# A selective scan whose step sizes return from DRAM already spread, in place of a spreading matmul

## The chip, the cores and the metric

One core of a Trainium2 chip. The metric is the device time of one execution in microseconds (us); lower is better.

## The reference

Eight images of 32x32 tokens with 192 channels pass through four residual blocks: attention with rotary positions (A), a selective scan (B), attention with relative positions (C) and 7x7 neighbourhood attention (D). The change is in B. What B computes, cut to the part that matters:

```python
x_dbl = jnp.einsum('bkdl,kcd->bkcl', xs, x_proj_w)        # xs: 4 directions over the 1024 tokens, 96 channels
dts, Bs, Cs = jnp.split(x_dbl, [R, R + N], axis=2)        # N = 16 states
dts = jax.nn.softplus(jnp.einsum('bkrl,kdr->bkdl', dts, dt_projs_w) + dt_projs_b[None, :, :, None])
def step(h, inp):                                          # over the 1024 tokens
    u_t, d_t, B_t, C_t = inp
    dA = jnp.exp(d_t[..., None] * As)
    h = h * dA + (d_t * u_t)[..., None] * B_t[:, :, None, :]
    y = jnp.einsum('bkcn,bkn->bkc', h, C_t)
```

## The kernel before

The four blocks run one after the other. In B the images also run one after the other. An image has a head (normalization, input projection, a 3x3 convolution, gates, then dt, B and C of the first direction), 48 tiles, and a tail (the sum over directions, a layer norm, a gate, the output projection).

A tile is 8 channels by 16 states on the 128 partitions, and all 1024 steps of the scan along the free axis. The 96 channels make 12 tiles for each direction k = 0 to 3; tile i has k, j = divmod(i, 12). For each tile:

- TensorE copies each of 8 rows of dt to 16 partitions (`spread_dt`, L1206 to L1219) into one of two slots of PSUM (`m.s2`), and the same for dt*u (`spread_du`, L1221 to L1230) into the single slot `m.s1`. A row is first split into a rounded part and a rest (`dth`, `duh`), so a spread has two parts and two halves: four matmuls.
- ScalarE takes the exponential of the spread dt in place in PSUM (L1376).
- VectorE multiplies the spread dt*u by B into `m.hs` in SBUF (`input_term`, L1478), then runs the scan (L1489): `h = h * dA + input`, with dA read from PSUM and the input from `hs`, written over `hs`.
- GpSimd multiplies the states by C (L1533) from SBUF into `m.hc`; every three tiles TensorE sums the 16 states back to channels in `m.px` (`fold`, L1232 to L1245).

The order on each engine is the program's order. VectorE runs `input_term(i + 1)` ahead of the scan of tile i. TensorE runs `spread_dt(i)`, waits until `input_term(i)` has emptied `m.s1`, and then runs `spread_du(i + 1)`; a slot of `m.s2` comes free when the scan that read it has ended. Between the tiles of direction k the work for direction k + 1 is threaded in: three projections on TensorE (tiles 0 to 5, also through `m.s1`), softplus on ScalarE (tiles 0 to 4) and on VectorE: `correct` (L1433) behind the scan of tile 5, `tail` (L1438) behind tile 6, `floor` (L1443) behind tile 7, `softplus` (L1448) and `scaled` (L1456, dt*u) behind tile 8, `low_dt` (L1461) behind tile 9, `low_du` (L1467) behind tile 10. All of these read two tensors from SBUF. ScalarE's `high_dt` and `high_du` (L1354, L1359) make the rounded parts. `m.dt` and `m.du` are the two halves of `m.xn`. SyncE's queue holds in B only the loads and stores of whole images.

Of the kernel before, what the change touches and what calls it, by code (L numbers as in the profile page):

```python
# [172 lines left out]
class ScanSignals:  # L173
    def __init__(self, sem, L):
# [23 lines left out]
        self.dt_ps = sem(f"{L}_dt_ps")  # L198
# [15 lines left out]
def allocate(nc, ctx):  # L214
# [106 lines left out]
    with ExitStack() as scan:  # L321
        m.dth = [sb(scan, f"dth{i}", [CP, 2, N], F32R) for i in range(2)]
# [862 lines left out]
def scan_image_tensor(nc, pe, m, b):  # L1185
# [20 lines left out]
    def spread_dt(i):  # L1206

        k, j = divmod(i, NG)
        if j == 0:
            pe.wait_ge(s.dt_lo, KD * b + k + 1)  # L1210
        if i == 1:
            pe.wait_ge(s.z_used, b + 1)
        if i >= 2:
            pe.wait_ge(s.h, TILES * b + i - 1)
        for f in range(NHF):
            for part in range(2):
                last = nc.tensor.matmul(m.s2[:, i % 2, f * HF:(f + 1) * HF], m.spread[:, ORDER[j], :],  # L1217
                                        m.dth[k % 2][:, part, f * HF:(f + 1) * HF], start=part == 0, stop=part == 1)
        last.then_inc(s.dt_ps, 1)  # L1219

    def spread_du(i, halves):  # L1221

        k, j = divmod(i, NG)
        if j == 0:
            pe.wait_ge(s.du_lo, KD * b + k + 1)
        for f in halves:
            for part in range(2):
                last = nc.tensor.matmul(m.s1[:, f, :], m.spread[:, ORDER[j], :],  # L1228
                                        m.duh[k % 2][:, part, f * HF:(f + 1) * HF], start=part == 0, stop=part == 1)
            last.then_inc(s.du_ps, 1)  # L1230
# [25 lines left out]
    spread_du(0, (0, 1))  # L1256
    for i in range(TILES):
        k, j = divmod(i, NG)
        spread_dt(i)
        pe.wait_ge(s.bt, TILES * b + i + 1)  # L1260
        f, ahead = j % 2, NHF * (KD * b + k + 1) + j % 2 + 1
        if k + 1 < KD and j < 2:
            project(k + 1, m.wdt, CP, f, s.dtp_ps)
            spread_du(i + 1, (1 - f,))
            pe.wait_ge(s.dtp_used, ahead)
            spread_du(i + 1, (f,))
        elif k + 1 < KD and j < 4:
            project(k + 1, m.xbw, P, f, s.brep_ps)
            spread_du(i + 1, (1 - f,))
            pe.wait_ge(s.brep, ahead)  # L1270
            spread_du(i + 1, (f,))
        elif k + 1 < KD and j < 6:
            project(k + 1, m.xcw, P, f, s.crep_ps)
            spread_du(i + 1, (1 - f,))
            pe.wait_ge(s.crep, ahead)
            spread_du(i + 1, (f,))
        elif i + 1 < TILES:
            spread_du(i + 1, (0, 1))
# [24 lines left out]
def scan_image_scalar(nc, act, m, b):  # L1303
# [64 lines left out]
    high_dt(0)  # L1368
# [3 lines left out]
    for i in range(TILES):  # L1372
        k, j = divmod(i, NG)
        act.wait_ge(s.dt_ps, TILES * b + i + 1)
        g = NG * k + ORDER[j]
        nc.scalar.activation(m.s2[:, i % 2, :], m.s2[:, i % 2, :], ACT.Exp,  # L1376
# [13 lines left out]
        if k + 1 < KD and j == 8:  # L1390
            high_dt(k + 1)
# [349 lines left out]
```

## Time and profile before

| | |
|---|---|
| median of 3 runs | 8861.15 us (8851.8 to 8868.71) |
| the profiled execution | 8870.59 us, span 8868.8 us, mean granted TensorE clock 0.864 |
| block B in it | the first scan at 1946.5, the last at 4528.6 us |
| one image of B | 334 us, of which 244.3 us from its first scan's start to its last scan's start |
| the scan instruction, L1489 | 384 times, 2277 ns each |
| GpSimd's multiply, L1533 | 384 times, 2551 ns each |

The span runs from the first to the last instruction. A row of the timeline has the start in us from the span's start, the duration in us, engine, line, operation and tiles; in brackets the idle time of the engine before it and who ended it. When an instruction had to wait for something that the profile doesn't record as a wait, its duration grows.

### The profile page before, as it was taken

How to read it: one execution, taken by the hardware profiler on the slowest of the kernel's cores; microseconds unless marked ns; L12 is line 12 of the kernel's file. 1: busy time of each engine (PE TensorE's matmuls, PEld its weight loads, DVE VectorE, ACT ScalarE, POOL GpSimd, SP SyncE). 2: the span in 40 equal slices, each digit the busy share in tenths (PEclk: the TensorE clock that was granted, in tenths of full speed). 3: DMA queues.
4: the chain of work that ended last, by engine and by line, in shares of the span. 5: the costliest groups of instructions: out<-in, count | busy, mean ns of one | idle time of the engine just before them, and what ended most of it. 6: DMA issues, size and time to landing. Idle time of an engine off the chain costs nothing. (4 is left out here: it accounts for less than half of the span.)

```text
span 8868.8 us, 86314 instructions
## 1 busy us (share of the span) xinstructions
PE 7117.3 (80%) x32664; PEld 2841.9 (32%) x32664; DVE 5281.6 (60%) x5310; ACT 3280.4 (37%) x3610; POOL 1168.2 (13%) x468
## 2 busy tenths in 40 slices
PE   6888888867777777777779999999989996777776
PEld 2222222223223223233234343344333432333332
DVE  5777777757777767777765555555555553333333
ACT  2555555532323322322323343333433432222222
POOL 0000000014334334334320000000000000000000
PEclk9999999988878778778778999999989997888787
DMA  2111111100000000000001001111010101222221
GB/s 65 47 46 48 48 48 48 46 23 0 7 7 0 7 7 0 7 7 0 4 29 29 27 29 35 29 30 30 27 35 27 30 25 54 65 66 62 64 68 46
DMA packets 152812, 282.83 MB, mean 32 GB/s; under 512 B 46858, under 2 KB 53762, under 8 KB 152398
## 3 DMA queue, kind: packets, MB, share of 16 engines
q1 hardware_dynamic: 152398, 277.31, 10.8%
q8 instruction: 260, 4.26, 0.2%
q14 instruction: 154, 1.26, 0.0%
HBM read 165.34 MB, written 89.79 MB: 29 GB/s over the span
## 5 line engine op out<-in xcount | busy, mean ns | idle before, releaser
L927 DVE TENSOR_REDUCE mx<-ring 128x1 f32<-128x1024 f32 (+1 forms) x1920 | 2187.8, 1141 | 2536.0 <-PE ring L674 1255.0
L825 ACT ACTIVATE pt<-ring 128x1024 f32<-128x1024 f32 (+1 forms) x1920 | 1868.4, 981 | 2836.0 <-PE ring L700 1329.5
L724 PE MATMUL px<-pt,vo 128*32 128x512 f32 (+3 forms) x8064 | 1277.2, 616 | 9.5 <-ACT pt L825 9.3
L671 PE MATMUL ring<-kb,qb 96*128 96x512 bf16 x3072 | 1121.2, 407 | 203.0 <-DVE rq L912 96.2
L698 PE MATMUL ring<-qb,kb 99*128 99x512 bf16 x3072 | 1124.0, 408 | 161.7 <-DVE nb L947 67.9
L1533 POOL TENSOR_TENSOR hc<-hs,crep 128x1024 f32<-128x1024 f32 x384 | 979.7, 2551 | 1684.0 <-DVE hs L1489 1593.7
L1228 PE MATMUL ring<-duh,spread 96*128 96x512 f32 x1536 | 650.7, 537 | 362.0 <-DVE hs L1478 230.5
L1489 DVE TENSOR_TENSOR_SCAN hs<-ring,hs 128x1024 f32<-128x1024 f32 x384 | 874.5, 2277 | 2.1 <-ACT ring L1376 2.1
L700 PE MATMUL ring<-rq,hot 128*128 128x512 f32 x1536 | 865.5, 622 | 0.0
L674 PE MATMUL ring<-hot,rq 128*128 128x512 f32 x1536 | 856.6, 616 | 0.0
L1376 ACT ACTIVATE ring<-ring,arow 128x1024 f32<-128x1024 f32 x384 | 415.9, 1083 | 947.8 <-PE ring L1217 947.8
L698 PEld LDWEIGHTS ring<-qb,kb 99*128 99x128 bf16 x3072 | 266.7, 100 | 1319.9 <-issue 684.5
L1478 DVE TENSOR_TENSOR hs<-ring,brep 128x1024 f32<-128x1024 f32 x384 | 467.3, 1217 | 358.8 <-PE ring L1228 312.6
L671 PEld LDWEIGHTS ring<-kb,qb 96*128 96x128 bf16 x3072 | 280.7, 100 | 907.0 <-issue 396.5
L1217 PE MATMUL ring<-dth,spread 96*128 96x512 f32 x1536 | 521.1, 467 | 30.4 <-DVE hs L1489 29.6
L667 PE MATMUL ring<-ks,qs 112*128 112x320 f32 x768 | 270.4, 441 | 330.5 <-DMA ks<-qk_split 295.2
L1228 PEld LDWEIGHTS ring<-duh,spread 96*128 96x128 f32 x1536 | 307.3, 218 | 699.8 <-DVE hs L1478 298.8
L1243 PE MATMUL px<-hc,fold 128*32 128x512 f32 x1536 | 476.0, 1018 | 31.8 <-POOL hc L1533 30.9
L1217 PEld LDWEIGHTS ring<-dth,spread 96*128 96x128 f32 x1536 | 313.4, 221 | 480.6 <-issue 346.4
L1030 POOL TENSOR_TENSOR ocn<-ocm,rb 96x1024 f32<-96x1024 f32 x24 | 56.7, 2362 | 2717.1 <-DMA rb<-reciprocals 2388.0
L1030 POOL TENSOR_TENSOR ocm<-ocm,rb 96x1024 f32<-96x1024 f32 x24 | 56.4, 2351 | 2428.2 <-DMA rb<-reciprocals 2428.2
L667 PEld LDWEIGHTS ring<-ks,qs 112*128 112x128 f32 x768 | 147.2, 234 | 609.5 <-issue 505.4
(169 smaller groups left out, 6792.5 us busy)
## 6 DMA issues: line engine op xcount, KB each, us to landing
qk_parts<-part SPq DMA_DIRECT2D x192, 192.0 KB, 2.4
qb<-qk_parts SPq DMA_DIRECT2D x192, 96.0 KB
kb<-qk_parts SPq DMA_DIRECT2D x192, 96.0 KB
ocm<-os SPq DMA_DIRECT2D x576, 32.0 KB
rb<-reciprocals SPq DMA_DIRECT2D x288, 64.0 KB, 2.5
qb<-qk_parts SPq DMA_DIRECT2D x192, 64.0 KB
kb<-qk_parts SPq DMA_DIRECT2D x192, 64.0 KB
qk_split<-hi SPq DMA_DIRECT2D x32, 384.0 KB, 3.5
```

What stands on the lines that cost most here:

```text
L671: last = nc.tensor.matmul(out[:, half], m.qb[u][0:BR, q], m.kb[u][0:BR, half], start=True, stop=L == "A")
L674: last = nc.tensor.matmul(out[:, half], m.rq[u][:, q], m.hot[:, half], start=False, stop=True)
L698: last = nc.tensor.matmul(out[:, half], m.kb[u][:, k], m.qb[u][:, half], start=True, stop=L == "A")
L700: last = nc.tensor.matmul(out[:, half], m.hot[:, k], m.rq[u][:, half], start=False, stop=True)
L724: last = nc.tensor.matmul(m.px[32 * g:32 * g + 32, h % 2, lo - f * HF:hi - f * HF], m.vo[img % 2][:, t, VW * head:VW * head + VC], pt[:, l ...
L825: nc.scalar.activation(pt, ps, ACT.Exp, scale=1.0 if L == "C" else HD ** -0.5).then_inc(s.pt, 1)
L927: nc.vector.tensor_reduce(out, ps, AX.X, ALU.max).then_inc(s.mx_used, 1)
L1217: last = nc.tensor.matmul(m.s2[:, i % 2, f * HF:(f + 1) * HF], m.spread[:, ORDER[j], :], m.dth[k % 2][:, part, f * HF:(f + 1) * HF], start ...
L1228: last = nc.tensor.matmul(m.s1[:, f, :], m.spread[:, ORDER[j], :], m.duh[k % 2][:, part, f * HF:(f + 1) * HF], start=part == 0, stop=part ...
L1243: last = nc.tensor.matmul(m.px[32 * band:32 * (band + 1), f, :], m.fold[:, v, :], rhs, start=False, stop=t >= TILES - BANDS, skip_group_ch ...
L1489: nc.vector.tensor_tensor_scan(m.hs[i % HSS][:], m.s2[:, i % 2, :], m.hs[i % HSS][:], 0.0, ALU.mult, ALU.add).then_inc(s.h, 1)
L1533: nc.gpsimd.tensor_tensor(m.hc[i % HCS][:], m.hs[i % HSS][:], m.crep[k % 2][:], ALU.mult).then_inc(s.hc, 1)
```

## The change

The spread of dt leaves TensorE. When softplus of a direction is done, SyncE writes dt (96 rows of 1024, 384 KB) to an internal DRAM tensor, waits until it has landed, and then issues one load for each tile: 8 rows, each read 16 times, 512 KB to 128 partitions of one of four new SBUF buffers `dts`. The load of tile i waits for the scan of tile i - 4. ScalarE's exponential works in place on `dts` in SBUF, and the scan reads dA from there. `high_dt`, `low_dt` and the buffers `dth` are gone; `low_du` moves from behind tile 10 to behind tile 9. The spread of dt*u takes over the two slots of `m.s2` and runs two tiles ahead; `m.s1` is left to the projections, which now wait only for the copy two projections back.

```diff
+DTS = 4
-        m.dth = [sb(scan, f"dth{i}", [CP, 2, N], F32R) for i in range(2)]
+        m.dts = [sb(scan, f"dts{i}", [P, N]) for i in range(DTS)]
+    m.dtd = nc.dram_tensor("dt_rows", (2, CP, N), F32, kind="Internal").ap()
...
-    def spread_dt(i):
+    def spread_du(i):
         k, j = divmod(i, NG)
         if j == 0:
-            pe.wait_ge(s.dt_lo, KD * b + k + 1)
+            pe.wait_ge(s.du_lo, KD * b + k + 1)
         if i == 1:
             pe.wait_ge(s.z_used, b + 1)
         if i >= 2:
-            pe.wait_ge(s.h, TILES * b + i - 1)
+            pe.wait_ge(s.bt, TILES * b + i - 1)
         for f in range(NHF):
             for part in range(2):
                 last = nc.tensor.matmul(m.s2[:, i % 2, f * HF:(f + 1) * HF], m.spread[:, ORDER[j], :],
-                                        m.dth[k % 2][:, part, f * HF:(f + 1) * HF], start=part == 0, stop=part == 1)
-        last.then_inc(s.dt_ps, 1)
-    def spread_du(i, halves):
...
                                         m.duh[k % 2][:, part, f * HF:(f + 1) * HF], start=part == 0, stop=part == 1)
-            last.then_inc(s.du_ps, 1)
+        last.then_inc(s.du_ps, 1)
...
-    spread_du(0, (0, 1))
+    for i in range(2):
+        spread_du(i)
     for i in range(TILES):
         k, j = divmod(i, NG)
-        spread_dt(i)
-        pe.wait_ge(s.bt, TILES * b + i + 1)
-        f, ahead = j % 2, NHF * (KD * b + k + 1) + j % 2 + 1
+        f, back = j % 2, NHF * (KD * b + k) + j % 2 + 1
         if k + 1 < KD and j < 2:
+            pe.wait_ge(s.crep, back)
             project(k + 1, m.wdt, CP, f, s.dtp_ps)
-            spread_du(i + 1, (1 - f,))
-            pe.wait_ge(s.dtp_used, ahead)
-            spread_du(i + 1, (f,))
         elif k + 1 < KD and j < 4:
+            pe.wait_ge(s.dtp_used, back + NHF)
             project(k + 1, m.xbw, P, f, s.brep_ps)
...
+        if i + 2 < TILES:
+            spread_du(i + 2)
...
-        act.wait_ge(s.dt_ps, TILES * b + i + 1)
+        act.wait_ge(s.dt_in[i % DTS], 16 * ((TILES * b + i) // DTS + 1))
         g = NG * k + ORDER[j]
-        nc.scalar.activation(m.s2[:, i % 2, :], m.s2[:, i % 2, :], ACT.Exp,
+        nc.scalar.activation(m.dts[i % DTS][:], m.dts[i % DTS][:], ACT.Exp,
                              scale=m.arow[:, g:g + 1]).then_inc(s.da, 1)
...
-        nc.vector.tensor_tensor(m.hs[i % HSS][:], flat(m.s1[:]), m.brep[k % 2][:], ALU.mult).then_inc(s.bt, 1)
+        nc.vector.tensor_tensor(m.hs[i % HSS][:], m.s2[:, i % 2, :], m.brep[k % 2][:], ALU.mult).then_inc(s.bt, 1)
...
-        nc.vector.tensor_tensor_scan(m.hs[i % HSS][:], m.s2[:, i % 2, :], m.hs[i % HSS][:], 0.0,
+        nc.vector.tensor_tensor_scan(m.hs[i % HSS][:], m.dts[i % DTS][:], m.hs[i % HSS][:], 0.0,
                                      ALU.mult, ALU.add).then_inc(s.h, 1)
...
         if k + 1 < KD and j == 9:
-            low_dt(k + 1)
-        if k + 1 < KD and j == 10:
             low_du(k + 1)
...
+        for i in range(TILES):
+            k, j = divmod(i, NG)
+            if j == 0:
+                sp.wait_ge(s.soft, 2 * (KD * b + k) + 1)
+                sp.dma_start(m.dtd[k % 2], m.dt[:]).then_inc(s.dt_out, 16)
+                sp.wait_ge(s.dt_out, 16 * (KD * b + k + 1))
+            if TILES * b + i >= DTS:
+                sp.wait_ge(s.h, TILES * b + i - DTS + 1)
+            rows = m.dtd[k % 2, DB * ORDER[j]:DB * (ORDER[j] + 1), :].rearrange("(d o) n -> d o n", o=1)
+            sp.dma_start(m.dts[i % DTS][:], rows.broadcast_to([DB, NS, N])).then_inc(s.dt_in[i % DTS], 16)
```

## Rows read from the trace of the kernel before

**Rows 1.** Windows, first image's tiles: us, busy of each engine, clock, DMA share, GB/s
```profile
1946.40:2190.70 244.30, 198.42 (x582) 85.84 (x582) 203.41 (x116) 80.91 (x85) 117.96 (x47) 0.83 0.00 0
```

**Rows 2.** Waits in the stretch 1940 to 2200: us in total, times, longest
```profile
DVE hs L1478 <- PE ring L1228: 38.9, 23, 3.6
```

**Rows 3.** Groups by line and shape, 1890 to 4250, the removed spread of dt
```profile
L1217 PE MATMUL ring<-dth,spread 96*128 96x512 f32 x1344 | 455.5, 467 | 26.8 <-DVE hs L1489 26.1
```

**Rows 4.** Timeline of the fourth direction, two scans beside a GpSimd multiply
```profile
2158.38 2.40 POOL L1533 TENSOR_TENSOR hc<-hs,crep 128x1024 f32<-128x1024 f32 x1 [0.85 <-DVE hs L1489]
...
2159.34 2.28 DVE L1489 TENSOR_TENSOR_SCAN hs<-ring,hs 128x1024 f32<-128x1024 f32 x1
...
2162.65 2.28 DVE L1489 TENSOR_TENSOR_SCAN hs<-ring,hs 128x1024 f32<-128x1024 f32 x1
```

**Rows 5.** Timeline of the first direction, tiles 5 to 9 and VectorE's work between them
```profile
1971.19 2.28 DVE L1489 TENSOR_TENSOR_SCAN hs<-ring,hs 128x1024 f32<-128x1024 f32 x1
...
1973.38 1.20 DVE L1433 SCALAR_TENSOR_TENSOR t<-t 96x1024 f32<-96x1024 f32 x1
...
1973.55 3.25 POOL L1533 TENSOR_TENSOR hc<-hs,crep 128x1024 f32<-128x1024 f32 x1 [2.88 <-DVE hs L1489]
...
1975.64 2.27 DVE L1489 TENSOR_TENSOR_SCAN hs<-ring,hs 128x1024 f32<-128x1024 f32 x1
...
1977.99 2.37 POOL L1533 TENSOR_TENSOR hc<-hs,crep 128x1024 f32<-128x1024 f32 x1 [1.19 <-DVE hs L1489]
1978.00 3.43 DVE L1438 TENSOR_TENSOR xn<-xn,t 96x1024 f32<-96x1024 f32 x1
...
1982.50 2.27 DVE L1489 TENSOR_TENSOR_SCAN hs<-ring,hs 128x1024 f32<-128x1024 f32 x1
...
1989.34 2.27 DVE L1489 TENSOR_TENSOR_SCAN hs<-ring,hs 128x1024 f32<-128x1024 f32 x1
...
1998.21 2.27 DVE L1489 TENSOR_TENSOR_SCAN hs<-ring,hs 128x1024 f32<-128x1024 f32 x1
```

**Rows 6.** Timeline of the second direction, the scans of its tiles 8 and 9
```profile
2055.57 2.27 DVE L1489 TENSOR_TENSOR_SCAN hs<-ring,hs 128x1024 f32<-128x1024 f32 x1
...
2063.73 2.27 DVE L1489 TENSOR_TENSOR_SCAN hs<-ring,hs 128x1024 f32<-128x1024 f32 x1
```

**Rows 7.** Timeline: scan of tiles 12, 36 and 47, and the copy that opens the tail
```profile
2014.71 2.28 DVE L1489 TENSOR_TENSOR_SCAN hs<-ring,hs 128x1024 f32<-128x1024 f32 x1
...
2152.71 2.28 DVE L1489 TENSOR_TENSOR_SCAN hs<-ring,hs 128x1024 f32<-128x1024 f32 x1
...
2190.68 2.29 DVE L1489 TENSOR_TENSOR_SCAN hs<-ring,hs 128x1024 f32<-128x1024 f32 x1 [0.27 <-ACT ring L1376]
...
2199.80 1.22 DVE L1506 COPY t<-px 96x1024 f32<-96x1024 f32 x1 [6.82 <-PE px L1243]
```

**Rows 8.** Timeline of the first image's head: softplus, a spread, a projection, the first scan
```profile
1932.69 1.22 DVE L1448 TENSOR_TENSOR xn<-xn 96x1024 f32<-96x1024 f32 x1
...
1938.31 2.05 PE L1228 MATMUL ring<-duh,spread 96*128 96x512 f32 x4 [4.75 <-DVE duh L1467]
...
1941.86 1.90 PE L1203 MATMUL ring<-u,wdt 96*96 96x512 f32 x2
...
1946.45 2.28 DVE L1489 TENSOR_TENSOR_SCAN hs<-ring,hs 128x1024 f32<-128x1024 f32 x1
```

**Rows 9.** DMA issues: KB each, median us from issue to landing
```profile
rb<-reciprocals SPq DMA_DIRECT2D x288, 64.0 KB, 2.5
...
qk_split<-hi SPq DMA_DIRECT2D x32, 384.0 KB, 3.5
...
x<-x_A SPq DMA_DIRECT2D x8, 768.0 KB, 5.4
```

**Rows 10.** Timeline of the first image's tail: two matmul groups of equal size
```profile
2201.07 1.96 PE L1287 MATMUL ring<-t,mean 96*96 96x512 f32 x4 [1.32 <-DVE t L1506]
...
2205.63 3.73 PE L1291 MATMUL ring<-xn,mean 96*96 96x512 f32 x4 [2.60 <-DVE xn L1511]
```

More of the change, by code:

```diff
@@ L189, in __init__ @@
         self.soft = sem(f"{L}_soft")
-        self.dt_hi = sem(f"{L}_dt_hi")
+        self.dt_out = sem(f"{L}_dt_out")
+        self.dt_in = [sem(f"{L}_dt_in{i}") for i in range(DTS)]
         self.du_hi = sem(f"{L}_du_hi")
-        self.dt_lo = sem(f"{L}_dt_lo")
         self.du_lo = sem(f"{L}_du_lo")
@@ L1217, in spread_dt @@
                 last = nc.tensor.matmul(m.s2[:, i % 2, f * HF:(f + 1) * HF], m.spread[:, ORDER[j], :],
-                                        m.dth[k % 2][:, part, f * HF:(f + 1) * HF], start=part == 0, stop=part == 1)
-        last.then_inc(s.dt_ps, 1)
-    def spread_du(i, halves):
[L1223 to L1228, printed above, removed]
                                         m.duh[k % 2][:, part, f * HF:(f + 1) * HF], start=part == 0, stop=part == 1)
-            last.then_inc(s.du_ps, 1)
+        last.then_inc(s.du_ps, 1)
     def fold(i, f):
@@ L1255, in scan_image_tensor @@
     pe.wait_ge(s.crep, NHF * KD * b + NHF)
-    spread_du(0, (0, 1))
+    for i in range(2):
+        spread_du(i)
     for i in range(TILES):
         k, j = divmod(i, NG)
-        spread_dt(i)
-        pe.wait_ge(s.bt, TILES * b + i + 1)
-        f, ahead = j % 2, NHF * (KD * b + k + 1) + j % 2 + 1
+        f, back = j % 2, NHF * (KD * b + k) + j % 2 + 1
         if k + 1 < KD and j < 2:
+            pe.wait_ge(s.crep, back)
             project(k + 1, m.wdt, CP, f, s.dtp_ps)
-            spread_du(i + 1, (1 - f,))
-            pe.wait_ge(s.dtp_used, ahead)
-            spread_du(i + 1, (f,))
         elif k + 1 < KD and j < 4:
+            pe.wait_ge(s.dtp_used, back + NHF)
             project(k + 1, m.xbw, P, f, s.brep_ps)
-            spread_du(i + 1, (1 - f,))
-            pe.wait_ge(s.brep, ahead)
-            spread_du(i + 1, (f,))
         elif k + 1 < KD and j < 6:
+            pe.wait_ge(s.brep, back + NHF)
             project(k + 1, m.xcw, P, f, s.crep_ps)
[L1274 to L1278, printed above, removed]
+        if i + 2 < TILES:
+            spread_du(i + 2)
         if i > BANDS and i % BANDS == 1:
@@ L1367, in scan_image_scalar @@
         copy_b(0, f)
-    high_dt(0)
     for f in range(NHF):
@@ L1389, in scan_image_scalar @@
             logarithm(k + 1)
-        if k + 1 < KD and j == 8:
-            high_dt(k + 1)
         if k + 1 < KD and j == 9:
@@ L1474, in input_term @@
             dve.wait_ge(s.brep, NHF * (KD * b + k + 1))
-        dve.wait_ge(s.du_ps, NHF * (TILES * b + i + 1))
+        dve.wait_ge(s.du_ps, TILES * b + i + 1)
         if i >= HSS:
             dve.wait_ge(s.hc, TILES * b + i - HSS + 1)
-        nc.vector.tensor_tensor(m.hs[i % HSS][:], flat(m.s1[:]), m.brep[k % 2][:], ALU.mult).then_inc(s.bt, 1)
-    for step in (correct, tail, floor, softplus, scaled, low_dt, low_du):
+        nc.vector.tensor_tensor(m.hs[i % HSS][:], m.s2[:, i % 2, :], m.brep[k % 2][:], ALU.mult).then_inc(s.bt, 1)
+    for step in (correct, tail, floor, softplus, scaled, low_du):
         step(0)
@@ L1561, in scan_sync @@
 def scan_sync(nc, sp, m):
+    s = m.s["B"]
     begin(sp, m, "B")
```

8 lines of the change are left out of this document (removed).

## The prediction

> **What bounds the kernel now.** The windows come first: they say which engine could be the bound in the tiles. In the 244.30 us of one image's tiles VectorE is busy 203.41, TensorE 198.42, GpSimd 117.96 and ScalarE 80.91 [rows 1]. No engine is full, so the order of waits sets the pace. The view of waits says which one: VectorE's `input_term` (L1478) waits for the spread of dt*u, 38.9 us in 23 waits [rows 2]. TensorE works through a spread of dt, a projection, a spread of dt*u and a fold in one line, and VectorE stands behind it. That is what the change attacks. The timeline then has to say what VectorE would do without that wait, and there two things are to be seen.
>
> First, VectorE's own floor. In the fourth direction, which has no projections and no softplus, two scans start 3.31 us apart (2159.34, 2162.65), and the GpSimd multiply that began at 2158.38 takes 2.40 us although a scan runs over half of it; the scan takes its usual 2.28 [rows 4]. The two engines don't disturb each other, and dA comes from PSUM there.
>
> Second, what happens when a VectorE instruction reads both its tensors from SBUF. `tail` (L1438) is issued at 1978.00, 0.01 us behind a GpSimd multiply of 2.37 us, and takes 3.43 instead of the 1.22 that the same kind takes when GpSimd is idle [rows 5, 8]. So it began in truth at 1978.00 + 3.43 - 1.22 = 1980.21, or 2.22 us behind the multiply's start: it waited the multiply out. `correct` (L1433) shows the other order: it began first (1973.38, 1.20 us), and the multiply behind it took 3.25 [rows 5]. The one that comes second waits for the whole of the first.
>
> **The change, part by part.**
>
> *The spread of dt on TensorE* goes: the 1344 matmuls of 336 tiles are 455.5 us busy [rows 3], 1.36 us for a tile, or 65 us for an image. With it goes `input_term`'s wait, since dt*u now runs two tiles ahead. By itself this would bring VectorE to its floor.
>
> *The scan now reads dA from SBUF, and `hs` from SBUF as before.* This makes it an instruction of the second kind. No row of before shows such a scan; the nearest rows are the two-input instructions of rows 5, and I take their behaviour for the scan: it waits for GpSimd's multiply. Every multiply starts as soon as a scan ends, always ahead of the next scan, because `input_term` (1.2 us, one input in PSUM) comes between. So a scan and a multiply can't overlap any more, and a tile costs their sum: from a scan's start to the multiply's start 1977.99 - 1975.64 = 2.35, and 2.22 from there until VectorE gets through: **4.57 us a tile**, where VectorE's floor is 3.31. The lower bound for a tile is that floor.
>
> The Trainium skill says the same of the port (page "SBUF — State Buffer", section "SBUF: two separate sides"): an instruction of VectorE with two SBUF inputs and a GpSimd instruction that reads SBUF exclude each other for the whole instruction, while one SBUF input doesn't contend. Rows 4 and 5 agree with both halves for other instructions; by the page the tile is 4.57 us, without it 3.31.
>
> *Tiles with direction work behind them.* Behind tile 5 (`correct`) and now behind tile 9 (`low_du`) VectorE comes first, and the multiply ends at 1973.55 + 3.25 = 1976.80; a waiting instruction gets through 0.15 before that end (1980.36 against 1980.21), so the next scan starts 1976.65 - 1971.19 = 5.46 us behind the last. In tiles 6, 7 and 8 multiply and softplus exclude each other already, and there nothing changes: 6.86, 6.84 and 8.87 us (8.16 in the second direction) [rows 5, 6]. The other seven tiles take 4.57. A direction with such work is then 7 x 4.57 + 2 x 5.46 + 6.86 + 6.84 + 8.87 = 65.5 us, the second 64.8: for three 195.7, against 2152.71 - 1946.45 = 206.3 before [rows 7, 8]. **Gain 10.5 us.** (The first alone: 68.3 before.)
>
> *The fourth direction*: ten tiles at 4.57, then 2.28 for the last, where no `input_term` stands between and VectorE comes first: 48.0 us, against 2190.68 - 2152.71 = 38.0 before. **Loss 10.0 us.** And in the tail one more multiply is still to be done behind the last scan: **loss 2.3 us**. The gain of three directions is spent in the fourth: + 1.8 us for an image.
>
> *TensorE under its new load.* Per tile a spread of dt*u is at most 2.05 us [rows 8]; with projection and fold some 5.3 at the lower clock in tiles 0 to 5 (1.9 for a projection [rows 8], the fold's 1.3 an estimate from the spread's four matmuls to its six in two of three tiles). That is over 4.57 by 0.7, 4.4 us over six tiles, hidden by two tiles' lead of over 7 us; without that cover it would be 4.4 us for a direction.
>
> *ScalarE* loses `high_dt`; its exponential (1.1 us) is hidden by three tiles. *`low_dt`* goes from VectorE; its 1.2 us for a direction are already in the sums above.
>
> *SyncE's queue* now holds 4 stores and 48 loads for each image, and even at 1 us of issue each that is 52 us in 334. Behind its wait for softplus stands the load of the next direction's tile 0. A load's landing: the broadcast of 64 KB takes 2.5 us, the image load of 768 KB 5.4 [rows 9], so 2.9 us for 704 KB; 512 KB on the same line lands in 4.3. Its source has only 8 rows; if that leaves half of the engines to it, the moving part doubles, and it is 6.2. I take 5.0. In mid-stream three tiles (13.7 us) cover it. At a change of direction softplus is done three scans before it is needed, some 17 us, against 3.5 (store [rows 9]) + 5.0 + 1.1: covered too; if not, up to 10 us for a direction.
>
> The Trainium skill (page "DMA: Bandwidth & Descriptors", section "Why a DMA increments its semaphore by 16 and not by 1") gives such a transfer 8 of the 16 engines, the count that divides both outermost dimensions. No row of before shows this; it would put the landing at the upper end.
>
> *The image's head* is where nothing hides the trip. Softplus ends at 1933.91; 0.15 + 3.5 for the store, 0.15 + 5.0 for the load, 1.1 for the exponential and 0.2 of handing over give the first scan at 1944.0, against 1946.45 [rows 8]. The other side, `scaled`, high and low part, two spreads of 2.05 and `input_term`, arrives at about 1943.2. **Gain 2.4 us** (3.1 to 1.2 for the landing's bounds).
>
> *The clock.* With about a third of its tile work gone TensorE may stand at the lower of its two levels (1.2 GHz) when the tail begins; there a group of four matmuls takes 3.73 instead of 1.96 [rows 10]. The head's matmuls are slow already. Between 0 and 1.8 us for an image; I take **0.9**.
>
> **The sum**: 1.8 - 2.4 + 0.9 = +0.3 us for an image, +2 us for eight. The profiled execution is 8870.59 us, 9.4 above the median of the runs, so I add to the median: 8861 + 2 = **8863 us**. A comparison here can tell some 0.2% (18 us) from no change. Forecast: no change that can be measured.
>
> **The rivals.**
>
> *The scan doesn't exclude the multiply.* It takes 2.28 us for 1024 elements where the two-input instructions of rows 5 take 1.2, and might fetch otherwise; against it, both kinds of two-input instruction here wait. Then seven tiles at 3.31, two at 4.45 and three unchanged make 54.6 us for a direction, and the fourth 35.4: some 45.7 us less for an image and 2.4 in the head: -385 us, about **8480**; nearer 8850 where transfers hold the tiles at 4.5. Chance 0.12.
>
> *The round trip in the head is late* (the rival on the slower side). Store, wait and load stand one behind the other with no cover, and 8 rows read 16 times each is a source not seen before. Each us beyond 5.0 costs 8 us in all; from a landing of 7.0 it decides. At 9 us: 8863 + 32 = **8895**. Chance 0.14.
>
> *The transfers set the pace.* 512 KB for each tile; if one took 6.2 us without overlap, 48 x 6.2 = 298 us for an image against 253: **9200**. It decides from 5.3 us a tile. For it: the doubt about the engines. Against: the image load moves more in 5.4. Chance 0.06.
>
> *My forecast*, exclusion and balance: 0.68. Its errors: 0.05 us on each of 37 tiles is 15 us; the head's landing 15 us; the clock 7. Its own range is 8838 to 8895, and in it 0.10 lies on the faster side beyond 0.2%, 0.42 within, 0.16 slower.
>
> Together: faster 0.12 + 0.10 = 0.22, same 0.42, slower 0.06 + 0.14 + 0.16 = 0.36. The range 8825 to 8920 leaves out the first and third rival.
>
> **What would show it.** Right: in the fourth direction scans start 4.6 us apart or are recorded at about 3.4 us instead of 2.28, the multiply beside them at 2.4, and `input_term` no longer waits for TensorE. The first direction takes about 65.5 us, the fourth 48. In the head the first scan starts 10.1 us behind softplus's end instead of 12.5. Wrong: scans of 2.28 us that overlap multiplies; the exponential waiting for a DMA in mid-stream; TensorE's waits back in front of `input_term`; a load's landing beyond 7 us.

## The result, and the profile after

The changed kernel takes **8896.5 us** (8889.2 to 8902.1, 7 runs) against 8861.15 us before (8851.8 to 8871.5, 7 runs): a ratio of **1.0040** (95% interval 1.0029 to 1.0052), 35 us slower. The prediction was 8863 us with a range of 8825 to 8920, so the range holds it. Of the three outcomes it had given 0.42 to "same" and 0.36 to "slower"; 35 us are more than the 18 that it took for no change, so by its own measure the kernel is slower. The profiled execution has a span of 8894.7 us (before 8868.8, 25.9 less) at a mean granted clock of 0.833.

The page of the changed kernel, its costliest groups. L1218 is the spread of dt*u, L1458 the scan, L1353 the exponential, L1447 `input_term`, L1500 GpSimd's multiply:
```profile
L1500 POOL TENSOR_TENSOR hc<-hs,crep 128x1024 f32<-128x1024 f32 x384 | 1055.2, 2751 | 1642.5 <-DVE hs L1458 1583.3
...
L1458 DVE TENSOR_TENSOR_SCAN hs<-dts,hs 128x1024 f32<-128x1024 f32 x384 | 1208.9, 3150 | 28.2 <-ACT dts L1353 28.2
...
L1353 ACT ACTIVATE dts<-dts,arow 128x1024 f32<-128x1024 f32 x384 | 438.4, 1147 | 807.3 <-DMA dts<-dt_rows 806.7
...
L1447 DVE TENSOR_TENSOR hs<-ring,brep 128x1024 f32<-128x1024 f32 x384 | 461.6, 1202 | 76.5 <-POOL hc L1500 50.3
```
A scan was 2277 ns and is 3150, a multiply was 2551 and is 2751. Nothing of 1024 elements became more work: the records contain waiting for each other. The exponential waits 807 us for loads. In the tiles this costs nothing, as loads at twice the rate will show; at the start of an image it does: there the scan waits for the exponential, 28.2 us in eight images.

The windows of the first image's tiles, as in [rows 1]:
```profile
1952.10:2201.50 249.40, 153.88 (x394) 54.14 (x392) 239.79 (x112) 80.32 (x83) 125.27 (x47) 0.70 0.40 103
```
TensorE fell from 198 to 154 us as meant. VectorE went from 203 to 240 of 249 us, so it is full now, and full of waiting that the profile doesn't call waiting. The clock in the tiles fell from 0.83 to 0.70. In the view of waits from 1940 to 2210 the wait that the change attacks, 38.9 us in [rows 2], has nearly gone, and another engine now stands in front of `input_term`:
```profile
DVE hs L1447 <- POOL hc L1500: 6.8, 3, 2.3
...
DVE hs L1447 <- PE ring L1218: 2.7, 2, 2.3
```
The timeline of the fourth direction, to be laid beside [rows 4]:
```profile
2169.17 2.38 POOL L1500 TENSOR_TENSOR hc<-hs,crep 128x1024 f32<-128x1024 f32 x1 [2.23 <-DVE hs L1458]
2170.13 3.58 DVE L1458 TENSOR_TENSOR_SCAN hs<-dts,hs 128x1024 f32<-128x1024 f32 x1
...
2173.63 1.19 DVE L1447 TENSOR_TENSOR hs<-ring,brep 128x1024 f32<-128x1024 f32 x1
2173.79 2.39 POOL L1500 TENSOR_TENSOR hc<-hs,crep 128x1024 f32<-128x1024 f32 x1 [2.23 <-DVE hs L1458]
2174.75 3.58 DVE L1458 TENSOR_TENSOR_SCAN hs<-dts,hs 128x1024 f32<-128x1024 f32 x1
```
The multiply keeps its 2.38. The scan is issued 0.96 behind it and recorded at 3.58, that is 2.28 of work behind 1.30 of waiting: it began in truth at 2171.43, 0.12 before the multiply's end (2171.55). Scans are 4.62 us apart, where they were 3.31.

The head, to be laid beside [rows 8]:
```profile
1940.26 1.22 DVE L1423 TENSOR_TENSOR xn<-xn 96x1024 f32<-96x1024 f32 x1
...
1941.51 0.31 SPq L1539 DMA_DIRECT2D dt_rows<-xn  x1
...
1944.49 2.66 SPq L1544 DMA_DIRECT2D dts<-dt_rows  x4
...
1950.86 1.15 ACT L1353 ACTIVATE dts<-dts,arow 128x1024 f32<-128x1024 f32 x1 [6.98 <-DMA dts<-dt_rows]
...
1952.12 2.29 DVE L1458 TENSOR_TENSOR_SCAN hs<-dts,hs 128x1024 f32<-128x1024 f32 x1 [1.82 <-ACT dts L1353]
```
The store has landed after 2.98 us (3.5 was taken), the load is waited for until 6.37 us after its issue (5.0 was taken, 6.2 was the upper bound). The first scan begins 10.64 us behind softplus's end; 10.1 was forecast and 12.5 it was before.

Last a change of direction, where the tiles don't take what was forecast. These are tiles 9, 10 and 11 of the first direction, VectorE and GpSimd only; they answer to the last row of [rows 5] and what follows it:
```profile
2003.21 2.27 DVE L1458 TENSOR_TENSOR_SCAN hs<-dts,hs 128x1024 f32<-128x1024 f32 x1
2005.41 1.19 DVE L1436 TENSOR_TENSOR duh<-xn,duh 96x1024 fp32r<-96x1024 f32 x1
2005.56 3.72 POOL L1500 TENSOR_TENSOR hc<-hs,crep 128x1024 f32<-128x1024 f32 x1 [6.48 <-DVE hs L1458]
2006.53 1.21 DVE L1447 TENSOR_TENSOR hs<-ring,brep 128x1024 f32<-128x1024 f32 x1
2007.66 3.76 DVE L1458 TENSOR_TENSOR_SCAN hs<-dts,hs 128x1024 f32<-128x1024 f32 x1
...
2011.35 1.19 DVE L1447 TENSOR_TENSOR hs<-ring,brep 128x1024 f32<-128x1024 f32 x1
2011.50 5.39 POOL L1500 TENSOR_TENSOR hc<-hs,crep 128x1024 f32<-128x1024 f32 x1 [2.23 <-DVE hs L1458]
2012.46 2.27 DVE L1458 TENSOR_TENSOR_SCAN hs<-dts,hs 128x1024 f32<-128x1024 f32 x1
...
2017.00 1.23 DVE L1447 TENSOR_TENSOR hs<-ring,brep 128x1024 f32<-128x1024 f32 x1 [2.26 <-POOL hc L1500]
```
The multiply of tile 9 lasts 3.72, not the 3.25 that one behind such an instruction takes in [rows 5]: it is late. Then the multiply of tile 10 is issued at 2011.50, 0.96 us ahead of the scan of tile 11, and still lets that scan go first: the scan has its 2.27, the multiply 5.39. I call these three tiles the disorder. The scan of tile 11 gains 1.3 us by that, and the next `input_term` (2017.00) waits for the late multiply, since it writes over the buffer `hs` that this multiply reads: there are three of them, and tile 13 has that of tile 10. From scan end to scan end tiles 9, 10 and 11 take 5.95, 3.31 and 6.62 us, in the second direction 6.67, 3.31 and 6.66 (means of eight images).

The budget, from the ends of the scans in both traces, in us for an image (mean of eight):

| part | predicted | before | after | measured |
|---|---|---|---|---|
| first three directions | -10.5 | 205.7 | 201.0 | -4.7 |
| fourth direction | +10.0 | 38.0 | 48.3 | +10.3 |
| last scan to the tail's copy | +2.3 | 6.8 | 8.8 | +2.0 |
| from u to the first scan's end | -2.4 | 33.3 | 31.3 | -1.9 |
| tail and head to the next u | +0.9 | 50.3 | 48.6 | -1.7 |

Eight times the first four lines and seven times the last are +34 us; outside of the block the profiled execution is 8 us shorter, which is no more than such executions differ among themselves, and the two make the 25.9 of the spans.

### The profile page after: what moved, and what is told of

Its sections match the earlier page's. It is cut to its first block and busy times, and to the rows that moved or that the text cites. A ratio compares the mean times of both kernels' runs of the same rounds, so it can differ in the third digit from the quotient of the medians.

```text
span 8894.7 us, 83593 instructions
## 1 busy us (share of the span) xinstructions
PE 6716.1 (76%) x31128; PEld 2582.3 (29%) x31128; DVE 5564.0 (63%) x5278; ACT 3262.8 (37%) x3578; POOL 1243.7 (14%) x468
## 3 DMA queue, kind: packets, MB, share of 16 engines
q14 instruction: 156, 1.28, 0.0%
## 5 line engine op out<-in xcount | busy, mean ns | idle before, releaser
L1500 POOL TENSOR_TENSOR hc<-hs,crep 128x1024 f32<-128x1024 f32 x384 | 1055.2, 2751 | 1642.5 <-DVE hs L1458 1583.3
L1218 PE MATMUL ring<-duh,spread 96*128 96x512 f32 x1536 | 659.8, 566 | 764.7 <-DVE hs L1447 492.5
L1458 DVE TENSOR_TENSOR_SCAN hs<-dts,hs 128x1024 f32<-128x1024 f32 x384 | 1208.9, 3150 | 28.2 <-ACT dts L1353 28.2
L1218 PEld LDWEIGHTS ring<-duh,spread 96*128 96x128 f32 x1536 | 356.9, 252 | 1309.8 <-DVE hs L1447 842.6
L1353 ACT ACTIVATE dts<-dts,arow 128x1024 f32<-128x1024 f32 x384 | 438.4, 1147 | 807.3 <-DMA dts<-dt_rows 806.7
L1233 PE MATMUL px<-hc,fold 128*32 128x512 f32 x1536 | 490.4, 1051 | 112.2 <-POOL hc L1500 110.7
L1447 DVE TENSOR_TENSOR hs<-ring,brep 128x1024 f32<-128x1024 f32 x384 | 461.6, 1202 | 76.5 <-POOL hc L1500 50.3
L701 PEld LDWEIGHTS ring<-rq,hot 128*128 128x128 f32 x1536 | 331.9, 216 | 0.0
L675 PEld LDWEIGHTS ring<-hot,rq 128*128 128x128 f32 x1536 | 326.8, 213 | 10.2 <-issue 9.3
```

Of the source, the lines that this page charges most:

```text
L675: last = nc.tensor.matmul(out[:, half], m.rq[u][:, q], m.hot[:, half], start=False, stop=True)
L701: last = nc.tensor.matmul(out[:, half], m.hot[:, k], m.rq[u][:, half], start=False, stop=True)
L1233: last = nc.tensor.matmul(m.px[32 * band:32 * (band + 1), f, :], m.fold[:, v, :], rhs, start=False, stop=t >= TILES - BANDS, skip_group_ch ...
L1458: nc.vector.tensor_tensor_scan(m.hs[i % HSS][:], m.dts[i % DTS][:], m.hs[i % HSS][:], 0.0, ALU.mult, ALU.add).then_inc(s.h, 1)
L1500: nc.gpsimd.tensor_tensor(m.hc[i % HCS][:], m.hs[i % HSS][:], m.crep[k % 2][:], ALU.mult).then_inc(s.hc, 1)
```

## The experiments

**One port or not: the scan's source alone.** The kernel before, with nothing changed but where dA lies.
```diff
+        m.ex = [sb(scan, f"ex{i}", [P, N]) for i in range(2)]
-        nc.scalar.activation(m.s2[:, i % 2, :], m.s2[:, i % 2, :], ACT.Exp,
+        nc.scalar.activation(m.ex[i % 2][:], m.s2[:, i % 2, :], ACT.Exp,
-        nc.vector.tensor_tensor_scan(m.hs[i % HSS][:], m.s2[:, i % 2, :], m.hs[i % HSS][:], 0.0,
+        nc.vector.tensor_tensor_scan(m.hs[i % HSS][:], m.ex[i % 2][:], m.hs[i % HSS][:], 0.0,
```


> The kernel before with one edit: the exponential writes dA to one of two SBUF buffers, so the scan reads both inputs from SBUF; TensorE still spreads dt, and no transfer is added. Theory (scan and GpSimd's multiply exclude each other): scans of the fourth direction go from 3.31 to 4.57 us apart (38 to 48 us), the tiles behind which VectorE has direction work gain about 1 us, the second direction's fast tiles rise to 4.57, and one multiply more stands in the tail: about +20 us for an image, +160 us in all, 1.8% slower than before. Rival (a scan may read both inputs beside the multiply): the same as before within 0.2%.

9012.5 us, ratio 1.0177 (1.0161 to 1.0193). In its fourth direction (timeline):
```profile
2170.45 2.39 POOL L1534 TENSOR_TENSOR hc<-hs,crep 128x1024 f32<-128x1024 f32 x1 [2.23 <-DVE hs L1490]
2171.41 3.58 DVE L1490 TENSOR_TENSOR_SCAN hs<-ex,hs 128x1024 f32<-128x1024 f32 x1
```
The same 3.58 as in the changed kernel, with dt still spread by TensorE and no DMA in the tiles. The tiles of an image take 261.2 us against 243.7, and the tail 2.0 more: 8 x 19.5 = 156 us, measured 152. Moving dA to SBUF costs this by itself. At the change to the second direction the multiplies last 3.27 and 3.26 (3.32 and 3.30 at the next): the disorder isn't there.

**The other half: dt from DRAM, dA in PSUM.** The changed kernel, but the exponential writes `m.s2`, and dt*u goes through the single slot `m.s1` one tile ahead, as before.
```diff
-        nc.scalar.activation(m.dts[i % DTS][:], m.dts[i % DTS][:], ACT.Exp,
+        nc.scalar.activation(m.s2[:, i % 2, :], m.dts[i % DTS][:], ACT.Exp,
-        nc.vector.tensor_tensor_scan(m.hs[i % HSS][:], m.dts[i % DTS][:], m.hs[i % HSS][:], 0.0,
+        nc.vector.tensor_tensor_scan(m.hs[i % HSS][:], m.s2[:, i % 2, :], m.hs[i % HSS][:], 0.0,
```


> The changed kernel's transfers of dt with the scan's operands of before: the exponential reads the loaded dt and writes dA to PSUM (m.s2), and the spread of dt*u goes through the single slot m.s1 again. Theory (exclusion is what spent the gain): no exclusion for scans, tiles at VectorE's floor of 3.31 us or at the transfers' pace of 4.08 us, whichever is longer; directions of some 56 us, the fourth at 12 x 4.08 = 49 us: about -33 us for an image against the changed kernel, 8630 us, 2.6% faster than before. Rival (transfers or TensorE's order set the pace, not the port): not faster than the kernel before.

8786.2 us, ratio 0.9919 (0.9905 to 0.9933). Scans are back at 2.28, and the multiplies beside them at 2.37. The sign is right, the size isn't, and the trace names two limits. In tiles 0 to 4 of the first and third directions scans end 5.1 to 5.5 us apart (3.9 to 4.7 in the second), and the timeline of the first shows why:
```profile
1954.18 1.22 DVE L1453 TENSOR_TENSOR hs<-ring,brep 128x1024 f32<-128x1024 f32 x1 [1.91 <-PE ring L1214]
...
1955.46 2.08 PE L1204 MATMUL ring<-u,xbw 96*128 96x512 f32 x2 [1.32 <-DVE hs L1453]
...
1957.58 0.60 ACT L1329 ACTIVATE brep<-ring 128x512 f32<-128x512 f32 x1 [2.21 <-PE ring L1204]
...
1959.48 1.22 DVE L1453 TENSOR_TENSOR hs<-ring,brep 128x1024 f32<-128x1024 f32 x1 [1.88 <-PE ring L1214]
```
`input_term`, projection, copy and the spread of half of dt*u stand in one line, because all go through one slot. In the fourth direction, from tile 4 on, the scan waits 0.9 us for the exponential, and that for its load: 3.9 us a tile.

**Where the order is lost, first theory: `low_du`.** The changed kernel with `low_du` back behind tile 10.
```diff
-        if k + 1 < KD and j == 9:
+        if k + 1 < KD and j == 10:
             low_du(k + 1)
```


> The changed kernel with low_du back behind tile 10. In the changed kernel tiles 9 to 11 of a direction take 15.9 to 16.6 us where 14.6 were expected, and GpSimd's multiplies of tiles 9 and 10 start late. Theory A (low_du or the spread that starts with it disturbs the multiply): the late multiplies move to tiles 10 and 11 or vanish. Theory B (the transfers of the new direction disturb it, 3.75 us behind the first load's issue): the multiply of tile 9 still ends at a fixed distance from that load, so tile 9 takes about 5 us, and tile 10 still sees a late one. Time: within 0.3% of the changed kernel either way.

8925.9 us, ratio 1.0074 (1.0061 to 1.0086). Tiles 9 to 11 take 3.31, 8.87 and 4.60. With nothing but `input_term` between scan 9 and scan 10, GpSimd's multiply of tile 9 still comes too late, and now by a whole scan:
```profile
2005.25 5.38 POOL L1500 TENSOR_TENSOR hc<-hs,crep 128x1024 f32<-128x1024 f32 x1 [6.48 <-DVE hs L1458]
2006.20 2.27 DVE L1458 TENSOR_TENSOR_SCAN hs<-dts,hs 128x1024 f32<-128x1024 f32 x1
```
`low_du` isn't the cause.

**Second theory: the store of dt and the loads behind it.** The store waits for the scan of tile 10.
```diff
             if j == 0:
                 sp.wait_ge(s.soft, 2 * (KD * b + k) + 1)
+                if k:
+                    sp.wait_ge(s.h, TILES * b + i - 1)
```


> The changed kernel with the store of dt held back until the scan of the direction's tile 10 has ended (for directions 2 to 4), so no transfer of the new direction runs beside the multiplies of tiles 9 and 10. Theory B (these transfers make the multiplies late): tile 9 takes 5.46 us, tile 10 4.6, and whatever is disturbed comes later, but the round trip (3.0 us store, 7 us first load) now stands in front of tile 12's scan: some 3 us later for each change of direction. Theory A (VectorE's or TensorE's work makes them late): tiles 9 and 10 stay at 5.95 and 3.31. Time: 0.2 to 1% slower than the changed kernel.

8975.2 us, ratio 1.0132 (1.0118 to 1.0146). The multiplies of tiles 9 and 10 still last 3.73 and 5.38, and in the 4 us around the first of them no transfer moves a byte (DMA share, last but one, and GB/s):
```profile
1999.60:2003.60 4.00, 2.76 (x7) 1.36 (x10) 4.00 (x4) 0.00 (x0) 3.73 (x1) 0.50 0.00 0
```
The transfers aren't the cause. Tile 11 takes 10.1 us instead of 6.6, for the round trip now lies open: 24 changes x 3.4 = 82 us, measured 79. That is also the price of the cover that the prediction had claimed for a change of direction, and had put at up to 10 us.

**Half of the engines.** The order of the 128 partitions is turned from 16 x channel + state to 8 x state + channel, by the constants, so that the load's outer dimension has 16 steps.
```diff
-            rows = m.dtd[...].rearrange("(d o) n -> d o n", o=1)
-            sp.dma_start(m.dts[i % DTS][:], rows.broadcast_to([DB, NS, N]))...
+            rows = m.dtd[...].rearrange("(o d) n -> o d n", o=1)
+            sp.dma_start(m.dts[i % DTS][:], rows.broadcast_to([NS, DB, N]))...
```


> The changed kernel with the 128 partitions of a tile ordered by state first (partition 8*state + channel instead of 16*channel + state), by the constants alone, so that the repeating dimension of the load of dt has 16 steps instead of 8. In the changed kernel a load of 512 KB takes 4.08 us back to back and its stretches show a DMA share near 0.5. Theory A (the eight steps put each load on half of the 16 engines, and the loads are hidden in mid-stream): the loads take about 2.1 us back to back, with a share near 0.9 while they run; tiles stay at 4.6 us, and only the first load of an image comes earlier, by 1 to 2 us; total 8 to 16 us below the changed kernel, 8880 to 8890. Theory B (the loads are bound by DRAM or by the write side, not by the number of engines): 4.08 us stays and the time stays at 8896. Rival on what sets the pace (the transfers set it in the changed kernel): tiles fall below 4.6 us and the total by over 100 us.

8880.0 us, ratio 1.0027 (1.0018 to 1.0037), 16.5 below the changed kernel. The windows of the same 8 us of the head, first of the changed kernel, then of this one; the last two columns are the DMA share and GB/s:
```profile
1949.00:1957.00 8.00, 8.00 (x20) 3.24 (x18) 5.23 (x4) 3.44 (x4) 2.38 (x1) 0.95 0.52 124
```
```profile
1949.00:1957.00 8.00, 8.00 (x19) 3.49 (x18) 7.59 (x5) 4.65 (x6) 2.39 (x1) 0.89 1.03 231
```
The same 512 KB moves at twice the rate. The tiles are the same (249.3 and 249.2 us), so the loads were hidden in mid-stream; the head is shorter, by 2.0 us (u to the first scan's end 29.3 against 31.3). 8 x 2.0 = 16, as measured. The way from the tail's copy to the next u is 1.4 us shorter too in this profiled execution, but not in that of the run with both repairs below, which has the same loads.

**The order forced, in two ways, and in one tile alone.** The scans of tiles 10 and 11 wait for the multiply of the tile before:
```diff
+        if k + 1 < KD and j >= 10:
+            dve.wait_ge(s.hc, TILES * b + i)
         nc.vector.tensor_tensor_scan(
```


> The changed kernel with one more wait: in the first three directions the scans of tiles 10 and 11 wait until GpSimd's multiply of the tile before has ended, as they in effect do at every other tile. In the changed kernel the three tiles 9 to 11 take 5.95, 3.31 and 6.62 us (15.9 together), with multiplies of 3.7 and 5.4 us. Theory A (the loss at tiles 9 to 11 is one of order: VectorE's scans get in ahead of GpSimd's multiplies, and the multiply that is late holds back the input term two tiles on): with the order forced the three take 5.5 to 5.7, 4.6 and 4.6, 14.8 together; 24 directions gain 1.1 us each, 25 to 28 us in all, 8870, about 1.001 against the kernel before. Theory B (something else stretches GpSimd's multiply there): the multiply of tile 9 stays at 3.7 us, the wait adds to it, and the total stays at 8896 or rises.

8878.5 us, ratio 1.0023 (1.0013 to 1.0032). Tiles 9 to 11 take 5.77, 4.87 and 4.58; the multiplies are 3.27 and 2.37 again. dA of tile 10 is as early here as in the changed kernel (1.20 us before scan 9 ends), so an early exponential by itself doesn't delay the multiply: it is late only where the scan behind it is free to go as well. Or dA of tiles 10 and 11 comes later:
```diff
+        if k + 1 < KD and j >= 10:
+            act.wait_ge(s.h, TILES * b + i)
         g = NG * k + ORDER[j]
```


> The changed kernel with the exponentials of tiles 10 and 11 of the first three directions held until the scan of the tile before has ended. This delays when the scan of tiles 10 and 11 can be asked for by some 1.2 us behind the end of the scan before, which is later than GpSimd's multiply asks. Theory A (GpSimd loses because the scan is ready ahead of it): the multiply of tile 9 and of tile 10 get in first, durations 3.3 and 2.4 us, tiles 9 to 11 take 5.5, 4.6 and 4.6 us, total 8870. Theory B (the order is fixed by something before it, as by low_du's arrival): the multiply of tile 9 stays at 3.7 us, and the time stays at 8896 within 5 us.

8872.5 us, ratio 1.0013 (1.0004 to 1.0022), 24 us below the changed kernel. No wait between VectorE and GpSimd was added, but the rows of tile 9 are different:
```profile
2009.74 1.21 DVE L1438 TENSOR_TENSOR duh<-xn,duh 96x1024 fp32r<-96x1024 f32 x1
2009.91 3.27 POOL L1502 TENSOR_TENSOR hc<-hs,crep 128x1024 f32<-128x1024 f32 x1 [6.48 <-DVE hs L1460]
2009.93 1.15 ACT L1355 ACTIVATE dts<-dts,arow 128x1024 f32<-128x1024 f32 x1 [2.33 <-DVE hs L1460]
2010.86 1.23 DVE L1449 TENSOR_TENSOR hs<-ring,brep 128x1024 f32<-128x1024 f32 x1
2011.99 3.34 DVE L1460 TENSOR_TENSOR_SCAN hs<-dts,hs 128x1024 f32<-128x1024 f32 x1
```
Tiles 9 to 11 take 5.50, 4.61 and 4.60, 14.7 in all; the prediction had 5.46 + 2 x 4.57 = 14.6. The tiles of an image take 245.15 us instead of 249.24. Is each early scan one that overtakes, or is the disorder handed on? The same with `j == 10` alone:

> The changed kernel with only the exponential of tile 10 held until the scan of tile 9 has ended; that of tile 11 is early, as in the changed kernel. Theory A (each scan whose dA is ready early overtakes the multiply by itself): tile 9 takes 5.5 us, but the multiply of tile 10 still loses to scan 11: tile 10 3.3, tile 11 6.6, together 15.4; 24 x 0.7 = 17 us above the version with both held, about 8885 to 8889. Theory B (the disorder starts with the late multiply of tile 9 and is handed on): with tile 9 in order tiles 10 and 11 take 4.6 each, together 14.7, and the time is that of the version with both held, 8872.

8872.0 us, ratio 1.0014 (1.0003 to 1.0024); tiles 5.51, 4.60, 4.60. It is handed on: with the multiply of tile 9 on time, tile 11's scan doesn't overtake, though its dA is ready 3.2 us before scan 10 ends. One wait in front of one exponential is the whole repair.

But ScalarE works in order, so this run held the exponential of tile 11 too, until after scan 9. Two more runs separate the two. Only tile 11's is held until scan 9 has ended:
```diff
+        if k + 1 < KD and j == 11:
+            act.wait_ge(s.h, TILES * b + i - 1)
```


> The changed kernel with only the exponential of tile 11 held until the scan of tile 9 has ended; that of tile 10 is as in the changed kernel, ready 1.2 us before the end of scan 9. In the changed kernel the exponentials of tiles 10 and 11 run back to back between the start and the end of scan 9, the second ends 0.16 us before the end of that scan. In the old kernel with dA in SBUF, where the order holds, dA of tile 10 is ready 1.24 us before that end too, but that of tile 11 only 4 us behind it. Theory A (dA of tile 10 being ready is what makes GpSimd's multiply late): nothing changes, tiles 9 to 11 take 5.95, 3.31, 6.62 us, 8896 us. Theory B (it is the exponential of tile 11, ready or ending beside the hand-over): the multiply of tile 9 takes 3.27, tiles 5.5, 4.6, 4.6, and the time is 8872 us.

8906.2 us, ratio 1.0037 (1.0023 to 1.0051); tiles 5.95, 3.31 and 6.63, as in the changed kernel. And the other way, both far earlier, with `high_du(k + 1)` behind `j == 11` instead of `j == 9`:

> The changed kernel with ScalarE's copy of the high part of dt*u moved from behind the exponential of tile 9 to behind that of tile 11. ScalarE then doesn't wait for the product in front of the exponentials of tiles 10 and 11, and both are done some 5 us or more before scan 9 ends, as they are in the fourth direction, where no multiply is late; no instruction of ScalarE but that copy is near the end of scan 9. Theory B1 (it matters that an exponential ends beside the hand-over, not that dA is early): the order holds, tiles 9 to 11 take 5.5, 4.6 and 4.6, 8872 us. Theory B2 (dA of two tiles ahead being ready is what disturbs, at this place): the multiplies stay at 3.7 and 5.4 us and the time at 8896.

8907.4 us, ratio 1.0040 (1.0026 to 1.0055), the same tiles again, with dA of tile 10 ready 12.7 us ahead of scan 9's end instead of 1.2:
```profile
2009.57 3.72 POOL L1500 TENSOR_TENSOR hc<-hs,crep 128x1024 f32<-128x1024 f32 x1 [6.48 <-DVE hs L1458]
```
So it is dA of tile 10, ready before the end of scan 9 (1.2 us or 12.7), and neither that of tile 11 nor an exponential that ends beside the hand-over.

**Both repairs together.** The waits in front of the exponentials of tiles 10 and 11, and the order of partitions that puts a load on 16 engines.

> The changed kernel with both single repairs together: exponentials of tiles 10 and 11 held until the scan before has ended (alone 8872.5 us, 24 us below the changed kernel) and the state-first order of partitions that puts a load on 16 engines (alone 8880.0, 16.5 below). Theory A (the two losses are separate, one at the changes of direction and one in the head): the gains add, 8896 - 24 - 16.5 = 8856 us, level with the kernel before (8860). Theory B (they share a cause, the timing of the loads against GpSimd's multiplies): the sum is less, 8865 to 8872, and the directions with the shorter transfers take other times than 65.8 us.

8857.6 us, ratio 0.9995 (0.9983 to 1.0007). They add. This is close to the kernel whose time the prediction had worked out: no disorder, and a first load that is used 4.4 to 5.0 us behind its issue, where the prediction took 5.0.

**A version that beats both.** dt from DRAM with loads on 16 engines, dA in PSUM, and the projections of B and C moved from tiles 2 to 5 to tiles 6 to 9:
```diff
-        elif k + 1 < KD and j < 4:
+        elif k + 1 < KD and j in (6, 7):
             project(k + 1, m.xbw, P, f, s.brep_ps)
...
-        elif k + 1 < KD and j < 6:
+        elif k + 1 < KD and j in (8, 9):
             project(k + 1, m.xcw, P, f, s.crep_ps)
```


> The kernel with dt loaded from DRAM, its exponential written to PSUM and du spread through the single slot (8786 us before), with two more edits: the state-first order of partitions, so that a load runs on 16 engines, and the projections of B and C for the next direction moved from tiles 2 to 5 to tiles 6 to 9, where VectorE's softplus steps make a tile 6.8 to 8.8 us long anyway. In the 8786 us version tiles 0 to 4 take 5.3 us on a chain of one slot: projection 2.1, copy 0.6, spread of half of du, input term 1.2. Theory A (that chain and the transfers' pace of 3.9 us set its tiles): tiles 2 to 5 fall to about 3.5 us, the fourth direction from 3.8 to about 3.4 us a tile, tiles 6 to 9 stay; 3 x 4 x 1.7 + 11 x 0.4 = 25 us an image, 200 us in all, about 8590. Theory B (another limit near 4.4 us stands behind, such as the chain of spread, input term and scan at a low TensorE clock): tiles 2 to 5 at 4.4 us, 3 x 4 x 0.9 + 4 = 15 us an image, 8665.

**8578.9 us**, ratio 0.9691 (0.9680 to 0.9703). In the first direction:
```profile
1963.60 2.36 POOL L1506 TENSOR_TENSOR hc<-hs,crep 128x1024 f32<-128x1024 f32 x1 [1.03 <-DVE hs L1464]
...
1964.63 2.28 DVE L1464 TENSOR_TENSOR_SCAN hs<-ring,hs 128x1024 f32<-128x1024 f32 x1
...
1968.03 2.28 DVE L1464 TENSOR_TENSOR_SCAN hs<-ring,hs 128x1024 f32<-128x1024 f32 x1
```
3.40 us a tile, 0.1 above VectorE's floor of 3.31. The tiles of an image take 211 us, those of the fourth direction 37.3.

## Why the prediction came out as it did

*The exclusion* was right, in place and size: 4.6 us a tile, recorded as a scan of 3.58. The kernel before with dA in SBUF shows it alone. It is what the Trainium skill states (page "SBUF — State Buffer", section "SBUF: two separate sides"), and the trace agrees for the scan. The rival that denied it (8480 us) falls.

*The fourth direction* (+10.0, measured +10.3) and *the tail's multiply* (+2.3, measured +2.0) were right.

*The first three directions* hold the term that was mis-sized, and with it most of the miss. Tiles 9 to 11, in its sum 5.46 + 4.57 + 4.57 = 14.6, measured 15.9, 16.6 and 15.9. That is 4.6 us for an image of the 5.8 by which this line missed; the remaining 1.2 are 4.61 instead of 4.57 in the other 15 tiles (0.6) and a mean image before that is 0.6 shorter than the one read in [rows 7]. The step that failed is "every multiply starts as soon as a scan ends, always ahead of the next scan". Which of the two goes first was taken from the starts in the timeline, and at tile 10 the scan goes first although the multiply was issued 0.96 us earlier. The runs that restore the order take 14.7 us there. In the tiles this is worth 8 x 4.1 = 33 us, while the two medians differ by 24. In the profiled executions the spans differ by 22.9: 8.3 of the 33 come back outside of block B, where the two kernels are the same, and 1.5 in heads and tails. Profiled executions differ by up to 20 us outside of B, so this is scatter and not a price.

*The head* was right in kind. The load took 6.37 instead of 5.0 to its use in the first image (6.4 to 7.3 in the eight), beyond the upper bound of 6.2, for it runs on half of the engines, the doubt that had set this bound; the store was 0.5 faster. A gain of 1.9 instead of 2.4, and the run on 16 engines gives 4.0. The Trainium skill (page "DMA: Bandwidth & Descriptors", section "Why a DMA increments its semaphore by 16 and not by 1") has the number of engines as the largest up to 16 that divides the outermost dimensions of both sides; a share of 0.52 with 8 steps and 1.03 with 16 agrees with it. The prediction named this and left it out of its sum. At 6.2 that sum would have been 8873. The rival of the late round trip didn't come true: with the faster store the trip costs 0.5 us an image more than forecast, and not 4.

*The transfers in mid-stream* were hidden: twice the rate leaves the tiles at 249.3, and the rival of 9200 us falls. *The cover at a change of direction* was there: when it is taken away, 3.4 us appear.

*The clock* had the wrong sign. The granted clock in the tiles fell to 0.70, but from the tail's copy to the next image's u it is 1.7 us less instead of 0.9 more. Of the groups in [rows 10] the first is 1.96 again and the second 3.46 in the mean of seven images (3.73 before); more than half of the gain is in the output projection behind them, 5.95 instead of 6.84. This is the second image, before and then after; TensorE's busy time is that projection, and the clock is third from the end:
```profile
2549.50:2557.50 8.00, 7.09 (x8) 2.09 (x8) 2.04 (x3) 0.00 (x0) 0.00 (x0) 0.56 0.00 0
```
```profile
2566.50:2574.50 8.00, 5.65 (x8) 1.85 (x8) 3.48 (x5) 0.00 (x0) 0.00 (x0) 0.71 0.00 0
```
The lighter load in the tiles isn't what does it: the kernel before with dA in SBUF, whose TensorE still has all its work, gains 1.5 us on the same way and has 5.98 for the projection. In both, two multiplies stand behind the last scan instead of one; whether that shifts the clock wasn't tried.

Two numbers of the prediction don't follow from its own working, and neither is in its sum. Six matmuls at a quarter of 2.05 us, in two of three tiles, make 2.05 us a tile for the fold and not 1.3; the measured 490.4 us in 384 tiles (L1233) are 1.28 all the same. And the third rival is held against 253 us for an image's tiles, where the prediction's own parts give 195.7 + 48.0 = 243.7.

In sum the forecast of a balance came out for a kernel without the disorder and with loads on all engines (8857.6 against 8863). The 35 us by which the changed kernel is slower come from two places: 8896.5 - 8857.6 = 39 us go when both are mended, 24 for the disorder and 16.5 for the half of the engines, taken one at a time. The head was nearly right in the forecast (0.5 us an image), so what it lacked is the disorder. That it missed by 33 us and no more is in part luck: the first three directions alone are 8 x 5.8 = 46 us off, and the clock's wrong sign took 7 x 2.6 = 18 back. Without that the time would have been about 8915, close to the range's end.

*Why* the multiply of tile 9 is late stays open. Shown is what it depends on: it is late when dA of tile 10 is ready before scan 9 ends, by 1.2 us or by 12.7, and on time when dA comes 1.2 us behind it; not on `low_du`, the transfers or tile 11. Not enough by itself is that dA is early: in the fourth direction it is, by 5.9 us, and no multiply is late; and in the kernel before with dA in SBUF dA of tile 10 is ready 1.24 us before scan 9 ends and the multiply takes 3.27. There dt*u for `input_term` is ready 0.07 us before that end, and in the changed kernel 8.9. But dA and dt*u both early aren't enough either. These rows are tile 5 of the second direction in the changed kernel, with dA of the next tile ready at 2038.61, 5.8 us before the scan ends at 2044.37, and dt*u earlier still:
```profile
2037.44 1.17 ACT L1353 ACTIVATE dts<-dts,arow 128x1024 f32<-128x1024 f32 x1 [0.44 <-DMA dts<-dt_rows]
...
2044.29 1.19 DVE L1408 SCALAR_TENSOR_TENSOR t<-t 96x1024 f32<-96x1024 f32 x1
2044.44 3.26 POOL L1500 TENSOR_TENSOR hc<-hs,crep 128x1024 f32<-128x1024 f32 x1 [2.23 <-DVE hs L1458]
```
An instruction of two inputs stands behind the scan as at tile 9, and the multiply is on time. One difference is left in view: that scan had itself been held up by a multiply (3.56), as were those of the fourth direction (3.58), and scan 9 had not (2.27). Whether this matters wasn't tried.

## What to carry to other kernels

Before an operand is moved, ask which memory the other inputs of its reader lie in: the same load of dt makes this kernel 0.8% faster with its exponential in PSUM (3.1% with the projections moved and all engines on the load), and 0.4% slower with it in SBUF. When a forecast is the difference of two large terms, the sign hangs on the smallest one that is off, so the irregular tiles (the changes of direction here) deserve the first doubt: a price carried over from regular tiles hid most of the miss. And a load that repeats few rows should have an outermost dimension that all engines can share; to order the partitions for it cost the tiles nothing here (249.3 us against 249.2).

## What was not expected of the hardware

The engine whose instruction is issued first doesn't always go first. At tile 10 the multiply was issued at 2011.50 and the scan at 2012.46, and the scan ran its plain 2.27 while the multiply took 5.39. The Trainium skill (page "SBUF — State Buffer", section "SBUF: two separate sides") says that whichever starts first has the shared pair of ports for its whole instruction. The trace agrees for what already runs (a scan beside a multiply is recorded at 3.58), but who starts first can't be read from the starts in the record. The durations tell it: the one that lasts its plain time went first. One exponential on ScalarE decided that order, and 24 us with it.
